# Five of the eight dense batches of expert 0 computed during the routing, in a two-layer transformer kernel

## The reference, cut to what matters

```
def _route(tokens, router_w):               # T = 4096 tokens, E = 8 experts, capacity 640
    probs = softmax(tokens @ router_w.T)
    top1_idx, top1_prob = argmax(probs), max(probs)
    ...                                     # within each expert the 640 tokens of highest probability
    keep = pos_in_group < capacity
    return where(keep, top1_idx, 0)         # the others fall back to expert 0

for e in range(E):
    h = relu(tokens @ W1[e] + b1[e])        # 128 -> 512
    y = h @ W2[e] + b2[e]                   # 512 -> 128
    out = out + where(final_e == e, y, 0)
```

## Time and profile before

| what | value |
|---|---|
| median of three runs | 1680.54 us (1679.21 to 1680.66) |
| profiled execution, its own time | 1676.52 us |
| its span, first to last instruction | 1674.7 us |
| TensorE / its weight loads busy | 1406.9 us (84%) / 1047.7 us (63%) |
| VectorE, ScalarE, GpSimd busy | 1084.9, 809.1, 667.2 us |
| mean granted TensorE clock | 0.935 |

### The profile page before, as it was taken

The page is one execution under the profiler, slowest core; times in us unless marked ns, Lnnn a source line. Parts: engine busy times, 40 slices in busy tenths (PEclk is TensorE's granted clock), DMA queues, the critical chain, the costliest instruction groups (busy, mean ns, idle before and its releaser), DMA issues. The chain is left out here.

```text
span 1674.7 us, 44899 instructions
## 1 busy us (share of the span) xinstructions
PE 1406.9 (84%) x14646; PEld 1047.7 (63%) x14646; DVE 1084.9 (65%) x3491; ACT 809.1 (48%) x2363; POOL 667.2 (40%) x1261
## 2 busy tenths in 40 slices
PE   4888888866869979999999999979999999966774
PEld 2666666655557746666666666657777777755662
DVE  3888888856410057877877877756777777762224
ACT  2555555531223337777777777744344344412330
POOL 1444444420523424444444444432234344444553
PEclk9999999975779979999999999989999999987887
DMA  5555633300111132122122122100000000003224
GB/s 191 167 173 173 217 113 107 109 1 1 38 43 45 37 103 74 57 73 73 57 73 71 58 73 70 60 19 1 1 10 11 11 13 13 12 28 79 76 72 158
DMA packets 89364, 115.46 MB, mean 69 GB/s; under 512 B 12418, under 2 KB 68746, under 8 KB 89168
## 3 DMA queue, kind: packets, MB, share of 16 engines
q1 hardware_dynamic: 82608, 102.55, 19.3%
q0 software_dynamic: 6688, 12.07, 2.2%
HBM read 78.97 MB, written 37.32 MB: 69 GB/s over the span
## 5 line engine op out<-in xcount | busy, mean ns | idle before, releaser
L1658 ACT ACTIVATE c_pr<-c_pS,c_nm 128x257 f32<-128x257 f32 x512 | 238.4, 472 | 97.7 <-DVE c_nm L1794 97.7
L1794 DVE TENSOR_REDUCE c_nm<-c_pS 128x1 f32<-128x257 f32 (+1 forms) x384 | 173.2, 505 | 42.6 <-PE c_pS L1538 42.5
L2110 ACT ACTIVATE s_k<-s_pK 128x512 f32<-128x512 f32 x128 | 76.4, 597 | 179.2 <-PE s_pK L2007 177.7
L1542 PE MATMUL c_pT<-cst,c_pr 128*128 128x128 f32 x1024 | 162.9, 284 | 0.0
L2007 PE MATMUL s_pK<-s_hT,AH 128*128 128x128 f32 x1024 | 138.6, 285 | 0.5 <-ACT s_hT L2105 0.5
L2007 PEld LDWEIGHTS s_pK<-s_hT,AH 128*128 128x128 f32 x1024 | 125.0, 196 | 21.4 <-ACT s_k L2110 18.2
L1542 PEld LDWEIGHTS c_pT<-cst,c_pr 128*128 128x128 f32 x1024 | 111.3, 141 | 37.7 <-issue 37.7
L2028 PE MATMUL s_pM<-BH,s_uT 128*128 128x128 f32 x1024 | 123.8, 280 | 5.0 <-DVE LG L2259 5.0
L2028 PEld LDWEIGHTS s_pM<-BH,s_uT 128*128 128x128 f32 x1024 | 119.5, 196 | 7.7 <-DVE LG L2259 7.7
L1803 DVE COPY c_prT<-c_pT 128x512 f32<-128x512 f32 x128 | 88.5, 692 | 23.9 <-PE c_pT L1542 18.5
L1538 PE MATMUL c_pS<-c_ks,c_qq 32*128 32x257 f32 x1024 | 92.7, 431 | 13.1 <-POOL c_qq L1710 8.0
(11 more groups left out here) (354 smaller groups left out, 3343.4 us busy)
## 6 DMA issues: line engine op xcount, KB each, us to landing
rows_in<-c_blank SPq DMA_DIRECT2D x32, 520.0 KB, 3.1
a_ctxT<-in_ctxT SPq DMA_DIRECT2D x32, 514.0 KB, 3.5
c_ctxT<-in_ctxT SPq DMA_DIRECT2D x128, 128.5 KB
a_ctxN<-in_ctxR SPq DMA_DIRECT2D x32, 512.0 KB, 4.1
f_back<-rows_out SPq DMA_DIRECT2D x24, 256.0 KB, 6.2
f_hb<-rows_in SPq DMA_DIRECT2D x39, 130.0 KB
f_w<-in_f_w SPq DMA_DIRECT2D x16, 256.0 KB, 3.4
rows_in<-a_zero SPq DMA_DIRECT2D x7, 322.5 KB, 4.5
```

The lines of the kernel that those rows point to most:

```text
L1542: mm = pe.transpose(pT[:, c, j, :], pr[:, b % 2, j, c * P:(c + 1) * P], k("ident"))
L1658: act.activation(pr[:, b % 2, c, :], pS[:, c, 0:S], ACT.Exp, bias=nm[:, c:c + 1], accum_out=den[:, b % 2, c:c + 1]).then_inc(e_ready.sem, 1)
L1794: dve.tensor_reduce(nm[:, c:end], pS[:, c:end, 0:S], AX.X, ALU.max, negate=True).then_inc(max_ready.sem, 1)
L2110: act.activation(k2[:, c * HK:(c + 1) * HK, :], pK[:, c % 2, :, :], ACT.Copy).then_inc(k_ready.sem, 1)
```

## The change

- `route_layer0` no longer makes the weight products. TensorE computes the first five dense batches of expert 0 there, in 40 pieces: an up piece is one 512-column matmul, a down piece is four matmuls for one group. `dense(8)` stands before the transposes of the probabilities, `dense(3)` or `dense(2)` follows each round's matmul, `dense(1)` follows the matmuls after the rounds. ScalarE takes the relus and copies each batch's result, unmasked, to the new SBUF tile y0. The three small results of routing share one PSUM bank.
- `experts_layer0` runs the three remaining dense batches, then the sorted experts, then the 14 weight pieces, which reuse hid and pH.
- VectorE no longer builds the bias of all tokens nor adds it in one instruction. After each sorted expert's add of b2 it adds five groups: from y0 under the mask (groups 0 to 19), and b2 of expert 0 under the mask.
- Token numbers become 32 t + g, so that `back` reads 2 KB per partition and transfer. `back` uses the memory of HT_all.
- wqkv and wout stay in SBUF through `experts_layer0`.

```
@@ build_program
         attend_layer0(env)
+        routed = ctx.enter_context(ExitStack())
+        env["y0"] = sb("y0", [P, DENSE * TG, D], c=routed)
         route_layer0(env)
+        experts_layer0(env)
+        routed.close()
         factors.close()
-        experts_layer0(env)
@@ attend_layer0
-            pool.iota(token[:, :], [[P, G]], base=0, channel_multiplier=1).then_inc(token_ready.sem, 1)
+            pool.iota(token[:, :], [[1, G]], base=0, channel_multiplier=G).then_inc(token_ready.sem, 1)
@@ route_layer0
+        pR = ctx.enter_context(nc.psum_tensor("r_pR", [P, 512], F32))
+        pP, pC, pB = pR[:, 0:N], pR[:, N:N + 16], pR[:, N + 16:N + 16 + G]
...
+            def hidden(n):
+                if n > 1:
+                    act.wait_ge(down_done.sem, n - 1)
+                for c in range(NF):
+                    m = n * NF + c
+                    act.wait_ge(up_done.sem, m + 1)
+                    act.activation(hid[:, n % 2, c, :], pH[:, m % 4, :], ACT.Relu, bias=vec[:, VB1_0 + c:VB1_0 + c + 1]).then_inc(up_ready.sem, 1)
+
+            hidden(0)
+            for n in range(DENSE):
+                if n + 1 < DENSE:
+                    hidden(n + 1)
+                act.wait_ge(down_done.sem, n + 1)
+                act.activation(y0[:, n * TG:(n + 1) * TG, :], pY[:, n % 2, :, :], ACT.Copy).then_inc(y0_ready.sem, 1)
...
+            def up(n, c):
+                m = n * NF + c
                 if m >= 4:
+                    pe.wait_ge(up_ready.sem, m - 3)
+                pe.matmul(pH[:, m % 4, :], w1[:, 0, c * P:(c + 1) * P], HT_all[:, n * TG:(n + 1) * TG, :].rearrange("p g t -> p (g t)"),
+                          start=True, stop=True).then_inc(up_done.sem, 1)
+
+            def down(n, i):
+                if i == 0:
+                    pe.wait_ge(up_ready.sem, (n + 1) * NF)
+                    if n > 1:
+                        pe.wait_ge(y0_ready.sem, n - 1)
+                for c in range(NF):
+                    mm = pe.matmul(pY[:, n % 2, i, :], hid[:, n % 2, c, i * P:(i + 1) * P], w2[:, 0, c, :],
+                                   start=(c == 0), stop=(c == NF - 1))
+                if i == TG - 1:
+                    mm.then_inc(down_done.sem, 1)
...
+            dense(8)
             pe.wait_ge(peers_ready.sem, 1)
             pe.wait_ge(pm_ready.sem, 1)
...
                 pe.matmul(pC[:, 0:4], peers[:, :], count[:, :], start=True, stop=True).then_inc(total_ready.sem, 1)
-                if n < PIECES - 1:
-                    weight_product(n + 1)
+                dense(3 if n % 3 == 0 else 2)
...
+            dense(1)
             pe.wait_ge(keep_ready.sem, 1)
...
+            pe.wait_ge(y0_ready.sem, DENSE)
@@ experts_layer0
-        def all_phases(dense, sorted_):
-
-            dense(0, BEFORE)
+        def all_phases(dense, sorted_, weights):
+
+            dense()
             sorted_()
-            dense(BEFORE, NB)
+            weights()
...
-                sp.dma_start(back[:, r, :], rows_out[n * N:(n + 1) * N, :].rearrange("(g p) d -> p g d", p=P)).then_inc(gathered[n], 16)
+                sp.dma_start(back[:, r, :], rows_out.rearrange("(p g) d -> p g d", g=G)[:, r, :]).then_inc(gathered[n], 16)
...
+            def weights():
+
+                pe.wait_ge(env["factors_loaded"], 32)
+                for m in range(PIECES):
+                    weight_product(m)
                 pe.wait_ge(y_ready, E - 1)
...
+            def weights():
                 act.wait_ge(y_done, E - 1)
+                for m in range(PIECES):
+                    act.wait_ge(piece_done, m + 1)
...
-            for g in range(G):
-                dve.tensor_scalar(bias[:, g, :], b2[:, 0, :], MASK[:, g, 0:1], None, ALU.mult).then_inc(bias_ready, 1)
-            dve.wait_ge(bias_ready, G)
-            dve.tensor_tensor(X[:, :, :], bias[:, :, :], X[:, :, :], ALU.add).then_inc(bias_ready, 1)
-            dve.wait_ge(bias_ready, G + 1)
...
+            def kept(first, end):
+                for g in range(first, min(end, DENSE * TG)):
+                    dve.scalar_tensor_tensor(X[:, g, :], y0[:, g, :], MASK[:, g, 0:1], X[:, g, :], ALU.mult, ALU.add).then_inc(y0_added, 1)
+                dve.wait_ge(y0_added, min(end, DENSE * TG))
+                dve.wait_ge(added, LATE * TG)
+                for g in range(first, min(end, G)):
+                    dve.scalar_tensor_tensor(X[:, g, :], b2[:, 0, :], MASK[:, g, 0:1], X[:, g, :], ALU.mult, ALU.add).then_inc(bias_ready, 1)
...
                     dve.tensor_tensor(y[:, e % 2, :, :], pY[:, :, :, :].rearrange("p i t d -> p (i t) d")[:, 0:NT, :],
                                       b2[:, e, :].unsqueeze(1).broadcast_to([P, NT, D]), ALU.add).then_inc(y_ready, 1)
+                    kept((e - 1) * AT_ONCE, e * AT_ONCE)
```

More of the change, by code:

```diff
@@ new lines, in _, with dense @@
+            given, LAST = [0], (2 * DENSE - 1) * NF
+            def dense(pieces):
+                for i in range(given[0], given[0] + pieces):
+                    n, j = divmod(i - NF, 2 * NF)
+                    if i < NF:
+                        up(0, i)
+                    elif i >= LAST:
+                        down(DENSE - 1, i - LAST)
+                    elif j < NF:
+                        up(n + 1, j)
+                    else:
+                        down(n, j - NF)
+                given[0] += pieces
@@ L1009, in experts_layer0 @@
     rows_in, rows_out, (w1, w2) = env["rows_in"], env["rows_out"], env["ew"][0]
+    AH, BH, gamma1, wqkv, wout, y0 = (env[n] for n in ("AH", "BH", "gamma1", "wqkv", "wout", "y0"))
     NF = F0 // P
@@ L1021, in experts_layer0 @@
         hid = sb("hid", [P, 2, NF, CAP])
[L1022 removed]
         h, hT, y = sb("h", [P, 2, NT, DR]), sb("hT", [P, 2, CAP]), sb("y", [P, 2, NT, D])
[L1024 removed]
+        back = HT_all
         token_of = sb("token_of", [P, E, NT], U32)
+        PIECES, AT_ONCE = 14, G // (E - 1) + 1
+        wT = hid[:, :, :, :].rearrange("p a c n -> p (a c n)")[:, 0:3 * RP * P].rearrange("p (a c n) -> p a c n", a=3, c=RP)
         pT = ps("pT", [P, 2, 512])
         pH = ps("pH", [P, 4, 512])
+        pW = pH[:, :, :].rearrange("p a (i n) -> p a i n", n=P)
         pY = ps("pY", [P, 2, 4, D])
@@ L1136, in sorted_, with weight_product, dense @@
                     sorted_down(e)
+            def weight_product(m):
+                if m >= 4:
+                    pe.wait_ge(piece_kept, 6 if 6 <= m < 10 else m - 3)
+                if m < 6:
+                    for i in range(4):
+                        c = (4 * (m % 2) + i) * P
+                        mm = pe.transpose(pW[:, m % 4, i, :], wqkv[:, m // 2, c:c + P], k("ident"))
+                else:
+                    n, odd = (m - 6) // 2, (m - 6) % 2
+                    r = slice(RH * odd, RH * odd + RH)
+                    for i in range(4):
+                        j = 4 * (n % 2) + i
+                        lhs, rhs = (wT[r, 1, j, :], wT[r, 0, j, :]) if n < 2 else (wT[r, 2, j, :], wout[r, j, :])
+                        mm = pe.matmul(pW[:, (m - 6) % 4, i, :], lhs, rhs, start=True, stop=True)
+                mm.then_inc(piece_done, 1)
+            def weights():
+                pe.wait_ge(env["factors_loaded"], 32)
+                for m in range(PIECES):
+                    weight_product(m)
                 pe.wait_ge(y_ready, E - 1)
-            all_phases(dense, sorted_)
+            all_phases(dense, sorted_, weights)
         @block.scalar
         def _(act):
-            def dense(first, end):
-                for n in range(first, end):
-                    if n > 1:
-                        act.wait_ge(down_done, n - 1)
+            def dense():
+                for r in range(LATE):
+                    if r > 1:
+                        act.wait_ge(down_done, r - 1)
                     for c in range(NF):
-                        m = n * NF + c
+                        m = r * NF + c
                         act.wait_ge(up_done, m + 1)
-                        act.activation(hid[:, n % 2, c, 0:N], pH[:, m % 4, :], ACT.Relu, bias=vec[:, VB1_0 + c:VB1_0 + c + 1]
+                        act.activation(hid[:, r % 2, c, 0:N], pH[:, m % 4, :], ACT.Relu, bias=vec[:, VB1_0 + c:VB1_0 + c + 1]
                                        ).then_inc(up_ready, 1)
```

107 lines of the change are left out of this document (45 added, 62 removed).

## The result

| | median us (runs) | ratio to before, 95% interval |
|---|---|---|
| before | 1680.51 (5) | 1 |
| after | 1668.81 (5) | 0.9934 (0.9917 to 0.9951) |
| after, again, beside before once more | 1668.72 (4), before 1679.14 (11) | 0.9945 (0.9925 to 0.9965) |

The change is 11.7 us faster by the first medians and 10.4 by the second (9.2 by the second ratio, whose interval goes from 5.9 to 12.6); 11.2 was forecast. The profiled execution took 1668.81 us (span 1667.0).

The account below looks back on a forecast made before the run. Routing's serial chain, then the scatters and a late TensorE, then two late dense batches were taken to bound the kernel. −12.0 (first sorted turn, routing included), +4 (cold start), −3.2 (tail) gave −11.2: 1669.3 us, range 1664 to 1685.

Parts of the forecast that it names:

- Routing: Routing stage: ends 5.2 us later, at 435.9, from front +4.3, rounds +2.4 and shorter small matmuls −1.5; bounds +2 to +38.8.
- Front: Start of routing: eight up pieces ahead of the transposes of the probabilities delay VectorE's copy, +4.3 us.
- rival 4: Routing: TensorE does not keep the high clock, up to +33.6 us on the forecast, 1702.9 (half of it 1686); chance 0.10.
- Long scatter gone: Expert stage: one scatter of 4.29 us, beside VectorE's whole-bias add, becomes 0.97 us, −3.3 us.
- First sorted turn at 483.0 for rows, cold, +4: First sorted expert: waits for rows and starts at 483.0, 12.0 us earlier; a low clock after idling costs +4.
- the crawl: Expert stage before the change, 462 to 480: TensorE does 19 matmuls in 18 us, cause unnamed; 20 us to spare would cover it.
- Rival 2: Routing or sorted experts: the slow TensorE stretch recurs uncovered, losing 15.8 us, so +4.6 in all, 1685.1; chance 0.10.
- one of my own signs of failure: First sorted expert: the prediction is wrong if its turn waits for TensorE rather than for rows.
- Tail: Behind the last expert: gather issued at 575.9, ends at 584.6, 11.2 us earlier, −3.2 in the sum; weight products done at 581.3.
- Rival 1: Tail: the weight pieces fall to 1.2 GHz, end 591.3, only 4.5 us earlier than before, 1676.0; chance 0.20.
- another of my signs of failure: Expert stage: the prediction is wrong if the slow TensorE stretch appears outside the three dense batches.
- Rival 3: Expert stage: the slow TensorE stretch belongs to the profiled execution alone, so the change brings +2.3, 1682.8; chance 0.10.

Follow-up runs that it names:

- b_noadd: Kernel before without the whole-bias add, the bias going to X in 32 short adds, five behind each sorted expert; ratio 1.0034 to before.
- the control: The kernel after, unchanged, run again beside other kernels on one chip; 1668.72 us, ratio 0.9945 to before.
- b_pause: Kernel before with four fills on GpSimd (5.3 us with waits) between scatters 16 and 17; ratio 0.9967 to before.
- a_late: Kernel after with all 32 scatters held back until VectorE has added the third dense batch; ratio 1.0052 to before.
- a_front4: Kernel after with four of the eight up pieces moved from ahead of the transposes to behind them; 1662.05 us, ratio 0.9912 to before.

## Why the prediction came out

The median came within 0.5 us of the forecast (1668.81 against 1669.3), by mechanisms that were half as told.

- **Routing, +5.2 told, +3.47 measured** (53.44 - 49.97). Front: +4.06 (told +4.3). The twelve round-to-round gaps: +0.87, the last steps -1.46 (told together +0.9): three-piece rounds cost 0.3 each, not 0.5, two-piece rounds gave 0.25 back, where 0.1 had been counted, and the first round took 2.0 us more than before, 1.6 of them because the clock had fallen. That the wide matmuls lift and hold the clock was right; rival 4 fell.
- **Long scatter gone, -3.3 told.** The train takes 40.8 us instead of 44.15: -3.36. The time did not fall by it, since the same edit moved the onset (b_noadd). By the Trainium skill, page "SBUF — State Buffer", section "Who interferes with whom", the 52 short adds should hold GpSimd too: of the scatters of an expert the first one or two, beside those adds, take up to 1.13 us instead of 0.97, and that is all that shows of the rule here: from the first y to the last takes 61.65 us, before 61.66.
- **First sorted turn at 483.0 for rows, cold, +4: the step that failed.** The rows were in by about 481 (load issued at 477.75, not 480.0; the last scatter ended at 476.44, and rows land 4.4 to 4.7 us behind that in the five kernels that wait for them). TensorE was late instead, until 486.79. I had said that 20 us to spare would cover the crawl of 18. It lasted 28, because the change had taken away the break that had put it off (b_noadd). What saved the sum is that a turn behind a busy TensorE pays no cold start, and that the rows were 2 us earlier than told: 483.0 + 4 and 486.79 are nearly the same time. That is luck, not working; with rows at 481 and a cold start of 3.1 to 4.2 the mechanism as told would have been about 2 us faster. The first y came 7.7 us earlier (7.9 in the control), told 8.0. Rival 2 in its mild form, and one of my own signs of failure, came true without moving the time.
- **Tail, -3.2 told, -1.6 measured** (last y to next stage 22.1 before, 20.54 after; 21.6 in the control, -0.5; -0.9 in the mean of the nine profiles with the 2 KB runs). This is the term whose size was wrong. The issue came 8.0 us earlier as told (7.6 from the start of the routing); the adds ended 10.15 us behind it instead of 8.7, as transfers landed. The row of layer 1 would have given 2.78 to the first add, not 1.2 plus one transfer. Rival 1 half came true: the clock was at 0.50 when the products began, behind TensorE's idle 5.82 us, though it had been 1.00 during the 24 transposes (565.99 to 571.35). Its price did not: the transposed pieces took 11 us instead of 4.8 to 6.5, held by ScalarE, but the eight products took 8.0 (577.16 to 585.16) and not 16.6: 1.02 us a piece at the clock of 0.50, and about 0.65 for the last four, when it had risen again (copies from 583.35 on). All 14 pieces took 20 us, between the 15 and the 25 told, and ended with the adds. That slow stretch beside the last scatters lies outside the three dense batches, which was another of my signs of failure, and no term of the sum had it.
- **Sum.** The stage is 9.3 us shorter in the profile of after and 8.6 in the control, against 11.2 told; the runs gave 11.7 and 10.4 by the medians. The time behind the stage varied from 1074 to 1080 us over the profiled kernels, which do not differ there, so the 2 us between are within what one execution tells; that the median met 1669.3 within 0.5 is partly chance.
- **Rival 3** (the crawl is of one profiled execution) fell: it is in every profile without a sufficient break, and b_pause and b_noadd moved the medians by it, 4.6 us down and 5.6 up.

**The crawl.** Shown: it comes beside a long train of scatters and not without one (a_late); the bytes that these write do not matter; in a train without a break it begins 15.1 to 18.0 us behind the first scatter (seven profiles), and a break puts it off by 2.2 to 3.8 us for each us; it takes hold of VectorE and ScalarE before TensorE, and full pace returns 2.5 to 5.3 us behind the last scatter. Not shown: what makes it, and whether anything fills up, as the backlog theory of the expectations has it. A burst of code loading it is not: from 453 to 476 the queue of instructions moved one packet in the kernel after; whether the engines lacked instructions was not tested. The Trainium skill, page "NOTIFIC — the notification-queue block", section "7.1 Overflow: three behaviours, one of which stalls the engine", has, as one of the settings of the path that carries trace records, that a full ring stalls their producer; no run here can show whether it is that.

## What to carry to other kernels

A stall that a change removes may have been protecting something: ask what ran undisturbed because of it, and look at every engine, not only at the one that was stalled. Where one stretch of a trace shows an engine at a tenth of its pace for no named reason, find on the chip what starts and ends it before a forecast counts it as covered; here two edits of a few lines each (a later train, a break in it) did that, though its cause is still open. And a busy engine that is a few us late can be worth as much as a punctual cold one, so a wait removed ahead of TensorE must be priced with the clock it leaves behind.

## What the hardware showed unexpectedly

- The crawl itself: single instructions of TensorE at steps of about 0.7 us or two or three times that, and of ScalarE up to 24 us apart, during 32 scatters of 1.28 us from start to start. In the tail ScalarE's copies came at 567.91, 570.03 and 572.20, in multiples of the same step, beside ten scatters in a row.
- The weight products, one piece a round, took 2.07 us each in routing. Back to back in the tail at the same 0.50 clock a piece takes 1.02 us (copies at 579.27, 580.29, 581.31). Successive pieces use the upper and the lower 64 rows in turn; the Trainium skill, page "TensorE: Matmul & The Clock Gate", section "Part 3: Packing small matmuls — row/col tiling", has matmuls of different row groups run at once, and the trace agrees: matmuls of two pieces start 0.04 us apart and take 0.42 us each:

```profile
581.62 0.42 PE L1183 MATMUL f_pH<-wout,f_hid 64*128 64x128 f32 x1
581.66 0.42 PE L1183 MATMUL f_pH<-f_hid 64*128 64x128 f32 x1
```

- In the seven profiles with eight ups ahead the clock fell for a moment right behind the transposes and an idle TensorE of 2.1 us (0.83 or 0.84 over 389 to 400, first round 4.6 us); in a_front4, with four ups behind them, it stayed at 1.00 there.
